# Batch 1's normalised input split in natural layout and turned by DMA; the first PSUM copies of batch 0 one weight part earlier

## The chip, the cores and the metric

The program runs on one core of one Trainium2 chip. The metric is the time of one execution on the device in microseconds (us): the median of the runs shown. One TensorE (PE), one VectorE (DVE), one ScalarE (ACT), one GpSimd (POOL) and one SyncE (SP) with its DMA queue take part. Every plain DMA of the kernel is issued by SP.

## The reference, cut to what matters

```python
x = L0_attn_x                                  # 2 x 1024 x 512, float32
xn = _layernorm(x, axis=-1)
q, k, v = proj(Wq), proj(Wk), proj(Wv)         # xn @ W.T, 16 heads of 32
scores = einsum(q, k) / sqrt(32), causal mask, softmax
s = (attn @ v) @ Wo.T
hidden = silu(xn @ W1.T) * (xn @ W3.T)         # 2048 wide
g = silu(fwht(hidden) @ W2.T)                  # Walsh-Hadamard along the last axis
out = x + s * g
```

## The kernel before, in words

The two batches run one after the other, each through `project`, `heads` and `tail`. Every engine's program is written out by hand, in its own order, and engines meet only through semaphores (`wait_ge`, `then_inc`). There is no scheduler: what stands in a function for an engine runs in that order on it.

float32 products are made of two parts, a high and a low one, so that each product is three matmuls (hi by hi, lo by hi, hi by lo; function `three`, L1585 to L1587, and L1617 for the first groups). In batch 0 the projections of q and k use parts in a rounded float32 form (`xt_hi`, `xt_lo`, `w_hi`, `w_lo`); the projection of v, the products with W1 and W3, and in batch 1 the projections of q and k too, use fp16 parts `x16_hi` and `x16_lo` (the trace calls them x_hi and x_lo), which hold 2048 times xn. They are laid out with the 512 features on partitions: [128, 4, 1024].

The normalised input `xb` [128 rows, 8 tiles, 512] is in natural layout. TensorE turns it: `transpose_xn(b, t)` (L1594) makes four transposes of 128x128 float32 for a tile of 128 rows, into a PSUM bank (`xt_bank(t)`: s0, s1 and the two banks of m). ACT then copies the bank to the high part (`xt` L879, `x16` L887), and DVE subtracts it from the bank for the low part (`xt` L1251, `x16` L1257). Eight tiles per batch, `t` 0 to 7.

`project(b)` on PE is `first_groups` (groups 0 and 1 of q, 24 matmuls), then groups 2 to 15 of q and k, each 12 matmuls of 512 columns, then 8 groups of v. Group `c` 0 reads tiles 0 to 3, group `c` 1 (from group 8 on) tiles 4 to 7. The first four tiles are transposed before the groups, tiles 4 to 7 after groups 4, 5 and 6 (`XT_AFTER`).

The down stage is the second half of `tail(b)`: for the 8 row tiles, `down(tp, i)` multiplies the hidden values of tile `2 * tp + i` with the transformed W2, 48 matmuls of 512 columns in two halves of 24 (`h` 0 and 1). A half can start when `h_lo_done[h]` says that its values are split. When PE has finished a half (`h_used[h]`), ACT makes the next tile's high part of it (`hidden_hi`, L1100) and DVE the low part (`hidden_lo`, L1487). After a tile's second half ACT and DVE finish the output rows (`gate` L1142, `finish` L1527 to L1534), SP stores them and loads the next rows of x. Between these, in batch 0, DVE makes the statistics and the normalisation of batch 1's input: `statistics` after places (0, 1) and (1, 1), `normalise` after (1, 0) and (2, 0), with `root` on ACT (`STATS_AT`, `NORM_AT`). Just before the last tile (7) of batch 0's down stage PE transposes tiles 0 to 3 of batch 1; ACT and DVE split Wq's four blocks and then these four tiles while PE is in that last tile.

At the start of batch 0, ACT splits the first three blocks of Wq, copies the four transposed tiles, and then splits the last block. PE's `first_groups` needs the high parts of all four tiles, then the low parts of all four.

Of the kernel before, what the change touches and what calls it, by code (L numbers as in the profile page):

```python
# [29 lines left out]
P = 128  # L30
# [3 lines left out]
KT = D // P  # L34
# [68 lines left out]
NORM_AT = [(1, 0), (2, 0)]  # L103

# [17 lines left out]
def build(nc, x, wq, wk, wv, wo, w1w3, w2, hadamard, out):  # L122
# [8 lines left out]
    with ctx:  # L131
# [105 lines left out]
        sb("room_after_g_lo0", [P, JT // 2, D], F16)  # L237
# [49 lines left out]
        x16_hi_done, x16_lo_done = sem("x16_hi_done"), sem("x16_lo_done")  # L287
        w13_scaled, w13_sum, w13_sum_ps, w13_scale_step, scan_in = sem("w13_scaled"), sem("w13_sum"), sem("w13_sum_ps"), sem("w13_scale_step"), [sem(f"scan_in{i}") for i in range(3)]
# [199 lines left out]
        def _(sp):  # L488
# [167 lines left out]
            def tail(b):  # L656
# [195 lines left out]
        def _(act):  # L852
# [28 lines left out]

            def x16(b, t):
                if b == 0:
                    act.wait_ge(xt_lo_done, t + 1)
                else:
                    act.wait_ge(xt_ps, b * NT + t + 1)
                act.activation(x16_hi[:, :, t * P:(t + 1) * P], xt_bank(t).rearrange("p (k c) -> p k c", k=KT),  # L887
                               ACT.Copy, scale=X_TOP).then_inc(x16_hi_done, 1)

            def project(b):  # L890
# [12 lines left out]
                if b == 0:  # L903
                    root(b, 0)
                    for i in range(KT - 1):
                        split_weight(b, i)
                    for t in range(TPC):
                        xt(b, t)
                    split_weight(b, KT - 1)
                for g in range(NQK):  # L910
# [6 lines left out]
                    for t in XT_AFTER.get(g, ()):  # L917
                        (xt, x16)[b](b, t)
# [177 lines left out]
            def tail(b):  # L1096
# [50 lines left out]
                for tp in range(NT // 2 - 1):  # L1147
                    for i in range(2):
                        hidden_hi(tp * 2 + (i + 1))
                        gate(tp, i)  # L1150
                        if b + 1 < B and (tp, i) in NORM_AT:
                            root(b + 1, NORM_AT.index((tp, i)))
                hidden_hi(NT - 1)
                gate(NT // 2 - 1, 0)
                if b + 1 < B:
# [4 lines left out]
                    for t in range(TPC):  # L1160
                        x16(b + 1, t)
# [17 lines left out]
        def _(dve):  # L1179
# [68 lines left out]
            def xt(b, t):  # L1248
# [3 lines left out]
                                  xt_hi[at].bitcast(F32), ALU.subtract).then_inc(xt_lo_done, 1)  # L1252

# [69 lines left out]
            def project(b):  # L1323
# [19 lines left out]
                for g in range(NQK):  # L1343
# [6 lines left out]
                    for t in XT_AFTER.get(g, ()):  # L1350
                        (xt, x16)[b](b, t)
# [131 lines left out]
            def tail(b):  # L1483
# [57 lines left out]
                for tp in range(NT // 2 - 1):  # L1541
                    for i in range(2):
# [4 lines left out]
                        if b + 1 < B and (tp, i) in NORM_AT:  # L1547
                            normalise(b + 1, NORM_AT.index((tp, i)))
                hidden_lo(NT - 1)
                finish(NT // 2 - 1, 0)  # L1550
                if b + 1 < B:
                    for i in range(KT):
                        split_weight(b + 1, i)
                    for t in range(TPC):
                        x16(b + 1, t)
# [25 lines left out]
        def _(pe):  # L1581
# [21 lines left out]
            def project(b):  # L1603
                def first_groups():

                    def products(g, p):
# [5 lines left out]
                        for kt in range(KT):  # L1612
# [19 lines left out]
                def group(g):  # L1632
# [5 lines left out]
                    if g < NQK:  # L1638
                        c, m, r = QK_GROUPS[g]
                        pe.wait_ge((xt_lo_done, x16_lo_done)[b], b * NT + (c + 1) * TPC)  # L1640
                        pe.wait_ge(split_lo, split_no(b, (m + 1) * KT))
                    else:
                        t = g - NQK
                        pe.wait_ge(wv_lo_done, (b + 1) * KT)
                        pe.wait_ge(x16_lo_done, x16_no(b, t))
# [17 lines left out]
                for g in range(2, NG):  # L1663
# [10 lines left out]
                    for t in XT_AFTER.get(g, ()):  # L1674
# [182 lines left out]
            def tail(b):  # L1857
# [73 lines left out]
                for tp in range(NT // 2):  # L1931
                    for i in range(2):
                        if b + 1 < B and tp * 2 + i == NT - 1:
                            pe.wait_ge(attn_done, (b + 1) * NT)
                            for t in range(TPC):
                                transpose_xn(b + 1, t)
# [44 lines left out]
```

## Time and profile before

| | us |
|---|---|
| median of 3 runs | 928.82 (928.81 to 930.75) |
| the profiled execution, its own time | 929.33 |
| its span in the trace | 927.6 |
| PE busy | 917.1 (99%), 6541 matmuls |
| DVE busy | 710.5 (77%) |
| ACT busy | 611.6 (66%) |
| POOL busy | 291.7 (31%) |
| DMA: 107.91 MB, share of 16 engines | 37.7% |
| granted TensorE clock | 0.999 |

The span runs from the first instruction to the last in the trace; the execution's own time is 1.7 us more. A matmul's record begins when it enters the array and lasts longer than the distance to the next one, so that distances between starts, not durations, say what a matmul costs PE. The batches divide the span so: batch 0's project to about 85 us, heads to 365, tail to 485 with its down stage from about 402 on; batch 1 from 485 on.

### The profile page before, as it was taken

Reading aid. Unit: us, or ns where it says so; the run is one execution under the profiler, and the core shown is the slowest. Engines: PE = TensorE matmul, PEld = TensorE weight load, DVE = VectorE, ACT = ScalarE, POOL = GpSimd, SP = SyncE. Lnnn points to the kernel's source line nnn. Section 1 sums busy time; section 2 is a strip of 40 time slices with the busy share of each in tenths; the row PEclk is TensorE's granted clock in tenths of the full one; section 3 lists DMA queues with packets and bytes.
Section 4 is the critical chain, followed back from the end, with each engine's and each line's share of the span. In section 5 each row is a group of like instructions: output and inputs, shape, how many; then the busy total and the mean of one; then the engine's idle time right before and its main releaser. Section 6 shows DMA issues by size and latency. Waiting matters only on the chain.

```text
span 927.6 us, 18915 instructions
## 1 busy us (share of the span) xinstructions
PE 917.1 (99%) x6541; PEld 528.1 (57%) x6541; DVE 710.5 (77%) x1413; ACT 611.6 (66%) x1281; POOL 291.7 (31%) x528
## 2 busy tenths in 40 slices
PE   8999999999999999999999999999999999999998
PEld 7864655665655656854444445555555555585445
DVE  7787999899899898766664569898989989843344
ACT  4558889998888877852443337788777887833231
POOL 1896664556556344000000002322323223310000
PEclk9999999999999999999999999999999999999999
DMA  9797356656346413672115411121211212150111
GB/s 292 277 254 257 104 156 171 177 143 163 107 120 168 125 48 99 232 256 84 46 57 176 134 38 42 47 75 42 82 41 58 64 41 65 46 205 23 46 46 46
DMA packets 64974, 107.91 MB, mean 116 GB/s; under 512 B 6640, under 2 KB 27760, under 8 KB 64368
## 3 DMA queue, kind: packets, MB, share of 16 engines
q1 hardware_dynamic: 64880, 106.72, 37.7%
q8 instruction: 52, 0.85, 0.4%
q14 instruction: 42, 0.34, 0.1%
HBM read 72.94 MB, written 33.55 MB: 115 GB/s over the span
## 4 chain that ended last, share of the span: by engine, by line
PE 71%; ACT 3%; DVE 2%; issue 1%; DMA 1%; POOL 0%; ACTq 0%; POOLq 0%; DVEq 0%
PE f L1801 25%; PE f L1586 7%; PE f L1585 7%; PE f L1587 7%; PE s L1758 5%; PE m L1738 3%; PE o L1776 3%; PE m L1881 3%; PE xs L1738 1%; PE o L1778 1%; PE m L1886 1%; DMA qk_st<-m_lo 1%; DVE p_lo L1417 1%; ACT stages L976 1%; PE s L1853 1%
## 5 line engine op out<-in xcount | busy, mean ns | idle before, releaser
L1417 DVE TENSOR_TENSOR p_lo<-stages,p_hi 128x512 f16<-128x512 f32 (+2 forms) x288 | 193.8, 681 | 22.1 <-ACT p_hi L986 21.2
L1801 PE MATMUL f<-x_hi,w_lo 128*128 128x512 f16 x512 | 194.6, 380 | 0.0
L1801 PE MATMUL f<-x_lo,w_hi 128*128 128x512 f16 x512 | 194.4, 380 | 0.0
L1801 PE MATMUL f<-x_hi,w_hi 128*128 128x512 f16 x512 | 193.9, 379 | 0.0
L986 ACT ACTIVATE p_hi<-stages 128x512 f16<-128x512 f32 (+2 forms) x288 | 160.2, 556 | 24.9 <-ACT stages L976 13.6
L777 POOL TENSOR_SCALAR_AFFINE_SELECT stages<-stages 128x128 f32<-128x128 f32 x192 | 68.3, 361 | 264.6 <-ACT stages L976 264.1
L1758 PE MATMUL s<-qk_st 98*128 98x512 f32 (+6 forms) x384 | 118.6, 383 | 1.2 <-ACT stages L976 0.3
L976 ACT ACTIVATE stages<-s,qk_back 128x512 f32<-128x512 f32 x144 | 88.2, 613 | 30.3 <-PE s L1758 29.5
L1400 DVE CUSTOM_DVE_ANT_0 m<-m,causal 128x1024 f32<-128x1024 f32 (+1 forms) x98 | 104.4, 1066 | 1.2 <-PE m L1738 1.2
L1100 ACT ACTIVATE h_hi<-hidden 128x1024 f16<-128x1024 f32 x32 | 33.9, 1058 | 95.8 <-PE f L1587 95.8
L1487 DVE TENSOR_TENSOR h_lo<-hidden,h_hi 128x1024 f16<-128x1024 f32 x32 | 39.2, 1224 | 75.1 <-ACT h_hi L1100 75.1
L1585 PE MATMUL f<-g_hi,h_hi 128*128 128x512 f16 (+1 forms) x256 | 95.4, 372 | 0.0
L1586 PE MATMUL f<-g_lo,h_hi 128*128 128x512 f16 (+1 forms) x256 | 95.3, 372 | 0.0
L1587 PE MATMUL f<-g_hi,h_lo 128*128 128x512 f16 (+1 forms) x256 | 95.3, 372 | 0.0
L976 ACT ACTIVATE stages<-s 128x512 f32<-128x512 f32 x144 | 75.5, 525 | 26.6 <-PE s L1758 25.7
L1738 PE MATMUL m<-qk_st 96*128 96x512 f32 (+7 forms) x256 | 79.4, 391 | 0.7 <-DVE mx L1400 0.7
L1801 PEld LDWEIGHTS f<-x_lo,w_hi 128*128 128x128 f16 x512 | 49.9, 97 | 52.3 <-issue 10.3
L1776 PE MATMUL o<-vparts,p_hi 128*128 128x65 f16 x1152 | 77.5, 190 | 0.1
L1801 PEld LDWEIGHTS f<-x_hi,w_lo 128*128 128x128 f16 x512 | 49.7, 97 | 47.3 <-issue 7.7
L1776 PEld LDWEIGHTS o<-vparts,p_hi 128*128 128x128 f16 x1152 | 71.7, 96 | 8.4 <-DVE p_lo L1417 0.2
L1778 PE MATMUL o<-vparts,p_lo 128*128 128x33 f16 x1152 | 76.2, 178 | 0.0
L1801 PEld LDWEIGHTS f<-x_hi,w_hi 128*128 128x128 f16 x512 | 50.5, 99 | 40.1 <-issue 3.7
(291 smaller groups left out, 1876.4 us busy)
## 6 DMA issues: line engine op xcount, KB each, us to landing
qk_st<-qk_parts SPq DMA_DIRECT2D x48, 256.0 KB, 4.6
w<-w1w SPq DMA_DIRECT2D x16, 512.0 KB, 4.3
scan<-w1w SPq DMA_DIRECT2D x12, 512.0 KB, 5.0
qk_st<-qk_parts SPq DMA_DIRECT2D x48, 128.0 KB, 2.6
wht_in<-w SPq DMA_DIRECT2D x4, 1024.0 KB, 10.9
qk_parts<-qk_hi SPq DMA_DIRECT2D x16, 256.0 KB, 3.2
qk_parts<-qk_lo SPq DMA_DIRECT2D x16, 256.0 KB, 4.9
w_butterflied<-wht_in SPq DMA_DIRECT2D x4, 1024.0 KB, 6.1
```

The lines of the kernel that those rows point to most:

```text
L976: act.activation(expd[q % NE][:, 0:end - need], SB[q % 2][:, 0, need - start:end - start], ACT.Exp, scale=1.0 if q < NH * NS else qk_back[ ...
L986: act.activation(p_hi[s][:], expd[q % NE][:, 0:end - need], ACT.Copy).then_inc(p_hi_done, 1)
L1400: dve.tensor_tensor_reduce(out=bank, in0=bank, in1=causal[:, S - width:S], scale=1.0, scalar=LOWEST, op0=ALU.add, op1=ALU.max, accum_out=m ...
L1417: dve.tensor_tensor(p_lo[s][:], expd[q % NE][:, 0:end - need], p_hi[s][:], ALU.subtract).then_inc(p_lo_done, 1)
L1585: pe.matmul(o, a_hi, b_hi, start=first, stop=False)
L1586: pe.matmul(o, a_hi, b_lo, start=False, stop=False)
L1587: return pe.matmul(o, a_lo, b_hi, start=False, stop=last)
L1738: mm = pe.matmul(bank[:, at:end], q[0:STACK, t * P:(t + 1) * P], k[0:STACK, at:end], start=True, stop=True)
L1758: pe.matmul(SB[q % 2][:, 0, 0:end - start], k_st[n // NH][n % NH % 3][0:STACK + 2, k * P:(k + 1) * P], q_st[n // NH][n % NH % 3][0:STACK + ...
L1776: pe.matmul(O[:, 0, first:first + VN], p_hi[s][:, at:at + P], v, start=k == 0 and t == c * TPC, stop=False, skip_group_check=True)
L1778: mm = pe.matmul(O[:, 0, first + DH:first + VN], p_lo[s][:, at:at + P], v[:, DH:VN], start=False, stop=t == k, skip_group_check=True)
L1801: mm = pe.matmul(F[m][:, 0, :], w, v, start=k == 0, stop=k == GMM - 1)
```

## The change

1. Batch 1's tiles are no longer transposed by PE, and its fp16 parts no longer made from PSUM. Instead ACT makes the high part in natural layout, `xn_hi` (`xn_high`), DVE the low part `xn_lo` (`xn_low`), and SP turns each with one transposing DMA of 128x512 fp16 into `x16_hi` and `x16_lo` (`turn_x16`): 16 such DMAs. Tiles 0 and 1 are made and turned after place (1, 1) of batch 0's down stage, 2 and 3 after (2, 0), 4 and 5 after (2, 1) (`TURN_AT`), 6 and 7 after the splits of Wq (`TURN_LAST`). The new buffers hold four tiles each, so that ACT waits for the turning of tiles 0 to 3 before it writes tile 4 (`x16_in[0]`).
2. In batch 0's start ACT splits two blocks of Wq ahead of its four copies instead of three, and PE goes through the hi-by-hi products of groups 0 and 1 block by block, in turn, before it asks for the low parts.

```diff
+TURN_AT = {(1, 1): (0, 1), (2, 0): (2, 3), (2, 1): (4, 5)}
+TURN_LAST = (6, 7)
+TURNED = 2 * TPC * 16
...
-        sb("room_after_g_lo0", [P, JT // 2, D], F16)
+        xn_hi = sb("xn_hi", [P, TPC, D], F16)
+        xn_lo = sb("xn_lo", [P, TPC, D], F16)
...
+                def turn_x16(t):
+
+                    sp.wait_ge(xn_lo_done, t + 1)
+                    for dst, src in ((x16_hi, xn_hi), (x16_lo, xn_lo)):
+                        sp.dma_start_transpose(dst[:, :, t * P:(t + 1) * P], src[:, t % TPC, :]
+                                               ).then_inc(x16_in[t // TPC], 16)
...
                     load_first(b + 1)
+                    sp.wait_ge(ffn_ps, (b + 1) * NH * GROUPS)
                 for tp in range(NT // 2 - 1):
                     for i in range(2):
                         store_y(tp, i)
                         load_x(tp * 2 + (i + 2), i)
+                        if b + 1 < B:
+                            for t in TURN_AT.get((tp, i), ()):
+                                turn_x16(t)
                 if b + 1 < B:
                     for i in range(5, NQ - 1):
                         load_weight(b + 1, i)
                 store_y(NT // 2 - 1, 0)
                 if b + 1 < B:
+                    for t in TURN_LAST:
+                        turn_x16(t)
                     store_y(NT // 2 - 1, 1)
...
+            def xn_high(t):
+
+                act.wait_ge(xn_done, NT + (t + 1))
+                if t >= TPC:
+                    act.wait_ge(x16_in[0], TURNED)
+                act.activation(xn_hi[:, t % TPC, :], xb[:, t, :], ACT.Copy, scale=X_TOP).then_inc(xn_hi_done, 1)
...
-                    for i in range(KT - 1):
+                    for i in range(2):
                         split_weight(b, i)
                     for t in range(TPC):
                         xt(b, t)
-                    split_weight(b, KT - 1)
+                    for i in range(2, KT):
+                        split_weight(b, i)
...
                         gate(tp, i)
                         if b + 1 < B and (tp, i) in NORM_AT:
                             root(b + 1, NORM_AT.index((tp, i)))
+                        if b + 1 < B:
+                            for t in TURN_AT.get((tp, i), ()):
+                                xn_high(t)
...
+            def xn_low(t):
+
+                dve.wait_ge(xn_hi_done, t + 1)
+                dve.scalar_tensor_tensor(xn_lo[:, t % TPC, :], xb[:, t, :], X_TOP, xn_hi[:, t % TPC, :],
+                                         ALU.mult, ALU.subtract).then_inc(xn_lo_done, 1)
...
                             normalise(b + 1, NORM_AT.index((tp, i)))
+                        if b + 1 < B:
+                            for t in TURN_AT.get((tp, i), ()):
+                                xn_low(t)
...
-                    for t in range(TPC):
-                        x16(b + 1, t)
+                    for t in TURN_LAST:
+                        xn_low(t)
...
-                    pe.wait_ge((xt_hi_done, x16_hi_done)[b], b * NT + TPC)
-                    products(0, 0)
-                    pe.wait_ge((xt_lo_done, x16_lo_done)[b], b * NT + TPC)
+                    if b == 0:
+                        pe.wait_ge(xt_hi_done, TPC)
+                    else:
+                        pe.wait_ge(x16_in[0], TURNED)
+                    for kt in range(KT):
+                        for g in range(2):
+                            products(g, 0, [kt])
+                    if b == 0:
+                        pe.wait_ge(xt_lo_done, TPC)
                     products(0, 1)
-                    products(1, 0)
                     products(1, 1)
...
-                        pe.wait_ge((xt_lo_done, x16_lo_done)[b], b * NT + (c + 1) * TPC)
+                        if b == 0:
+                            pe.wait_ge(xt_lo_done, (c + 1) * TPC)
+                        else:
+                            pe.wait_ge(x16_in[c], TURNED)
...
                             pe.wait_ge(attn_done, (b + 1) * NT)
-                            for t in range(TPC):
-                                transpose_xn(b + 1, t)
```

Where the diff cuts lines, ACT's and DVE's loops over `XT_AFTER` and PE's `transpose_xn` in them now run for batch 0 alone, and the last two tiles' `xn_high` stands on ACT where `x16` of four tiles stood.

On PE, at the border between tiles 6 and 7 of batch 0's down stage, before:

```order
L1587 MATMUL f<-g_hi,h_lo 128x512
L1594 MATMUL s<-ident,xb 128x128 x8
L1594 MATMUL m<-ident,xb 128x128 x8
L1585 MATMUL f<-g_hi,h_hi 128x512
L1586 MATMUL f<-g_lo,h_hi 128x512
```

The two L1594 rows (four tiles, 16 transposes) are gone now, and so are the three places with 4, 4 and 8 of them in batch 1's project; tile 7's matmuls follow on tile 6's.

On DVE, in the down stage from place (1, 1) to the splits of Wq, before:

```order
L1223 BN_STATS stats<-xb 128x6 x4
L1487 TENSOR_TENSOR h_lo<-hidden,h_hi 128x1024 x2
...
L1245 TENSOR_SCALAR xb<-xb,mv,rstd 128x512 x4
L1487 TENSOR_TENSOR h_lo<-hidden,h_hi 128x1024 x2
L1527 SCALAR_TENSOR_TENSOR y<-y,f 128x512
L1530 TENSOR_TENSOR y<-y,ctx_nat 128x512
L1534 SCALAR_TENSOR_TENSOR y<-y,g_back,x_in 128x512
L1487 TENSOR_TENSOR h_lo<-hidden,h_hi 128x1024 x2
```

and now (its own line numbers):

```order
L1250 BN_STATS stats<-xb 128x6 x4
L1284 SCALAR_TENSOR_TENSOR xn_lo<-xb,xn_hi 128x512 x2
L1520 TENSOR_TENSOR h_lo<-hidden,h_hi 128x1024 x2
...
L1272 TENSOR_SCALAR xb<-xb,mv,rstd 128x512 x4
L1284 SCALAR_TENSOR_TENSOR xn_lo<-xb,xn_hi 128x512 x2
L1520 TENSOR_TENSOR h_lo<-hidden,h_hi 128x1024 x2
L1560 SCALAR_TENSOR_TENSOR y<-y,f 128x512
L1563 TENSOR_TENSOR y<-y,ctx_nat 128x512
L1567 SCALAR_TENSOR_TENSOR y<-y,g_back,x_in 128x512
L1284 SCALAR_TENSOR_TENSOR xn_lo<-xb,xn_hi 128x512 x2
L1520 TENSOR_TENSOR h_lo<-hidden,h_hi 128x1024 x2
```

Three times, two low parts now stand ahead of the low part of the next hidden tile, on the engine that PE waits for at each half; on ACT two high parts stand in the same three places ahead of the next `h_hi`.

On PE, the first groups of batch 0, now:

```order
L1630 MATMUL m<-ident,xb 128x128 x8
L1637 MATMUL f<-ident 128x128 x6
L1653 MATMUL f<-xt_hi,w_hi 128x512
L1653 MATMUL o<-xt_hi,w_hi 128x512
...
L1653 MATMUL f<-xt_lo,w_hi 128x512 x4
L1653 MATMUL o<-xt_lo,w_hi 128x512 x4
L1653 MATMUL f<-xt_hi,w_lo 128x512 x4
L1653 MATMUL o<-xt_hi,w_lo 128x512 x4
```

where before four of `f<-xt_hi,w_hi`, four of `f<-xt_lo,w_hi` and only then four of `o<-xt_hi,w_hi` came: eight matmuls instead of four now stand ahead of the first that needs a low part.

## Rows read from the trace of the kernel before

**Rows 1.** The page: busy time and share of each engine.

```profile
PE 917.1 (99%) x6541; PEld 528.1 (57%) x6541; DVE 710.5 (77%) x1413; ACT 611.6 (66%) x1281; POOL 291.7 (31%) x528
```

**Rows 2.** 10 us of the down stage: length; busy PE, PEld, DVE, ACT, POOL; PEclk, DMA, GB/s.

```profile
460.00:470.00 10.00, 10.00 (x48) 4.47 (x46) 5.79 (x7) 4.09 (x4) 0.00 (x0) 1.00 0.11 31
```

**Rows 3.** Timeline of PE around the transposes: start us, us, engine, line, instruction, count.

```profile
472.62 0.38 PE L1587 MATMUL f<-g_hi,h_lo 128*128 128x512 f16 x1
472.83 1.04 PE L1594 MATMUL s<-ident,xb 128*128 128x128 f32 x8
473.71 1.04 PE L1594 MATMUL m<-ident,xb 128*128 128x128 f32 x8
474.58 0.38 PE L1585 MATMUL f<-g_hi,h_hi 128*128 128x512 f16 x1
474.80 0.38 PE L1586 MATMUL f<-g_lo,h_hi 128*128 128x512 f16 x1
...
500.70 0.38 PE L1587 MATMUL o<-x_hi,w_lo 128*128 128x512 f16 x1
500.92 0.60 PE L1594 MATMUL s<-ident,xb 128*128 128x128 f32 x4
501.35 0.38 PE L1585 MATMUL xs<-x_hi,w_hi 128*128 128x512 f16 x1
...
503.94 1.04 PE L1594 MATMUL m<-ident,xb 128*128 128x128 f32 x8
504.82 0.38 PE L1585 MATMUL f<-x_hi,w_hi 128*128 128x512 f16 x1
```

**Rows 4.** Timeline of PE at the start: the first groups, 24 matmuls to group 2.

```profile
12.43 1.19 PE L1617 MATMUL f<-xt_hi,w_hi 128*128 128x512 f32 x4
13.48 1.21 PE L1617 MATMUL f<-xt_lo,w_hi 128*128 128x512 f32 x4
...
18.19 0.39 PE L1585 MATMUL xs<-xt_hi,w_hi 128*128 128x512 f32 x1
18.42 0.39 PE L1586 MATMUL xs<-xt_lo,w_hi 128*128 128x512 f32 x1
```

**Rows 5.** Timeline of ACT and DVE at the start.

```profile
8.51 1.92 ACT L857 ACTIVATE w_hi<-stages 128x512 fp32r<-128x512 f32 x3 [0.35 <-DMA stages<-wq]
9.02 1.92 DVE L1245 TENSOR_SCALAR xb<-xb,mv,rstd 128x512 f32<-128x512 f32 x4
...
12.15 1.28 DVE L1251 TENSOR_TENSOR xt_lo<-m,xt_hi 128x512 fp32r<-128x512 f32 x2
12.24 0.65 ACT L857 ACTIVATE w_hi<-w 128x512 fp32r<-128x512 f32 x1
```

**Rows 6.** Timeline of DVE in the down stage.

```profile
449.55 1.21 DVE L1487 TENSOR_TENSOR h_lo<-hidden,h_hi 128x1024 f16<-128x1024 f32 x1
...
460.15 1.22 DVE L1487 TENSOR_TENSOR h_lo<-hidden,h_hi 128x1024 f16<-128x1024 f32 x1
...
477.37 2.07 DVE L1188 SCALAR_TENSOR_TENSOR w_lo<-stages,qk_scale,w_hi 128x512 f16<-128x512 f32 x3
```

**Rows 7.** Timeline of PE where the next half of the hidden values begins.

```profile
452.11 0.38 PE L1585 MATMUL f<-g_hi,h_hi 128*128 128x512 f16 x1
...
462.47 0.38 PE L1585 MATMUL f<-g_hi,h_hi 128*128 128x512 f16 x1
```

**Rows 8.** Timeline of ACT in the down stage.

```profile
465.04 0.69 ACT L1142 ACTIVATE y<-f,g_back 128x512 f32<-128x512 f32 x1
467.85 1.06 ACT L1100 ACTIVATE h_hi<-hidden 128x1024 f16<-128x1024 f32 x1 [2.12 <-PE f L1587]
...
475.44 1.95 ACT L859 ACTIVATE w_hi<-stages,qk_scale 128x512 f16<-128x512 f32 x3 [0.77 <-issue]
```

**Rows 9.** DMA issues: count, KB each, median us from issue to landing.

```profile
qk_parts<-qk_lo SPq DMA_DIRECT2D x16, 256.0 KB, 4.9
qk_parts<-qk_hi SPq DMA_DIRECT2D x16, 128.0 KB, 1.7
```

More of the change, by code:

```diff
@@ L287, in build @@
         x16_hi_done, x16_lo_done = sem("x16_hi_done"), sem("x16_lo_done")
+        xn_hi_done, xn_lo_done, x16_in = sem("xn_hi_done"), sem("xn_lo_done"), [sem(f"x16_in{i}") for i in range(NC)]
         w13_scaled, w13_sum, w13_sum_ps, w13_scale_step, scan_in = sem("w13_scaled"), sem("w13_sum"), sem("w13_sum_ps"), sem("w13_scale_step"), [sem(f"scan_in{i}") for i in range(3)]
@@ L880, in xt @@
                                ACT.Copy).then_inc(xt_hi_done, 1)
+            def xn_high(t):
[3 more added lines that the diff above has]
+                act.activation(xn_hi[:, t % TPC, :], xb[:, t, :], ACT.Copy, scale=X_TOP).then_inc(xn_hi_done, 1)
             def x16(b, t):
[L883 to L886, printed above, removed]
+                act.wait_ge(xt_lo_done, t + 1)
                 act.activation(x16_hi[:, :, t * P:(t + 1) * P], xt_bank(t).rearrange("p (k c) -> p k c", k=KT),
@@ L916, in project @@
                         root(b, 1)
-                    for t in XT_AFTER.get(g, ()):
-                        (xt, x16)[b](b, t)
+                    if b == 0:
+                        for t in XT_AFTER.get(g, ()):
+                            xt(b, t)
                     if g - 1 in WV_AT:
@@ L1159, in tail @@
                         split_weight(b + 1, i)
-                    for t in range(TPC):
-                        x16(b + 1, t)
+                    for t in TURN_LAST:
+                        xn_high(t)
                 if b + 1 < B:
@@ L1349, in project @@
                         normalise(b, 1)
-                    for t in XT_AFTER.get(g, ()):
-                        (xt, x16)[b](b, t)
+                    for t in XT_AFTER.get(g, ()) if b == 0 else ():
+                        xt(b, t)
                     for t in X16_AFTER.get(g, ()) if b == 0 else ():
@@ L1553, in tail @@
                         split_weight(b + 1, i)
-                    for t in range(TPC):
-                        x16(b + 1, t)
+                    for t in TURN_LAST:
+                        xn_low(t)
                 if b + 1 < B:
@@ L1604, in first_groups, with products @@
                 def first_groups():
-                    def products(g, p):
+                    def products(g, p, kts=range(KT)):
                         r = QK_GROUPS[g][2]
@@ L1611, in products @@
                             w, v = (w16_hi, w16_hi, w16_lo)[p][0], (x16_hi, x16_lo, x16_hi)[p]
-                        for kt in range(KT):
+                        for kt in kts:
                             if g == 0 and p == 0:
@@ L1644, in group @@
                         pe.wait_ge(wv_lo_done, (b + 1) * KT)
-                        pe.wait_ge(x16_lo_done, x16_no(b, t))
+                        if b == 0:
+                            pe.wait_ge(x16_lo_done, x16_no(b, t))
                     for kt in range(KT):
@@ L1673, in project @@
                     group(g)
-                    for t in XT_AFTER.get(g, ()):
+                    for t in XT_AFTER.get(g, ()) if b == 0 else ():
                         transpose_xn(b, t)
@@ L1934, in tail @@
                             pe.wait_ge(attn_done, (b + 1) * NT)
-                            for t in range(TPC):
-                                transpose_xn(b + 1, t)
                         if b + 1 == B and tp * 2 + i == NT - 1:
```

1 line of the change is left out of this document (added).

## The prediction

> **What bounds the kernel.** I read the page's first part, then busy time by stretches, then the timelines of single engines at the places that the change touches. TensorE is busy 917.1 of 927.6 us [rows 1], and in the down stage, where most of the change lies, all 10.00 of 10.00 us at full clock, with DVE, ACT (5.79 and 4.09 us) and the DMA engines (0.11) mostly free [rows 2]. So whatever leaves TensorE's program shortens the kernel by its own time, as long as no other engine then comes late at one of TensorE's waits. The reader should see two things: what a row costs TensorE is the distance between starts, 0.22 us for a matmul of 512 columns [rows 3], and the waits that can come late are those for `h_lo`, since DVE and ACT get new work ahead of them.
>
> **Part 1, what is removed from TensorE.** Four tiles stood between 472.83 and 474.58, after a matmul begun at 472.62. From there to 474.58 are 1.96 us, of which 0.22 belong to the matmul: 1.74 us for 16 transposes [rows 3]. A place with four of them costs 501.35 - 500.70 - 0.22 = 0.43 us, and there are two of these (after groups 4 and 5; the other reads the same); the place with eight costs 504.82 - 503.94 = 0.88 us [rows 3]. The sum is 1.74 + 2 x 0.43 + 0.88 = 3.48 us. The 16 copies by ACT and subtractions by DVE from PSUM go with them, and 16 of like size from SBUF come: ACT about 0.65 us each and DVE about 0.66 us each, by the split of Wq with the same types (1.95 and 2.07 us for three) [rows 6, 8].
>
> **Where they come, DVE.** Twice two low parts, 1.32 us, go in front of an `h_lo` half that TensorE wants soon. At place (1, 1) `h_lo` began at 449.55 and took 1.21 us; with 1.32 us more it ends at 452.08. The half's first matmul began at 452.11, and its weight load, which is what waits, about 0.1 us ahead of it: TensorE comes some 0.1 us late [rows 6, 7]. At (2, 0), 460.15 + 1.32 + 1.22 = 462.69 against 462.47: 0.2 us, with the load's lead and some 0.05 us for the semaphore 0.4 us late [rows 6, 7]. Together I take +0.5 us; the ends are 0 (if operands from SBUF go at half that time) and +1.3 us (if each low part costs a quarter more, which adds 0.33 us in each of the two places). At (2, 1) and after the splits of Wq the pieces have microseconds to spare. On ACT the high parts at (1, 1) and (2, 0) are ahead of DVE's own chain and cost nothing.
>
> **Part 1, the transposing DMAs.** The trace of before has none, so their cost is bounded. What hides them is the down stage's 10.4 us per tile. The tight one is ACT's wait for the turning of tiles 0 to 3 before it writes tile 4, since ACT then owes TensorE the next `h_hi`. Tiles 2 and 3 are ready to be turned at 460.15 + 1.32 = 461.5 (tile 2 a little before) [rows 6]. TensorE wants tile 7's first half at 472.7, where it used to begin the transposes [rows 3]. Back from there: `h_lo` 1.21, `h_hi` 1.06, two high parts 1.3: the four DMAs must have landed by 469.1, 7.6 us after 461.5 [rows 3, 6, 8]. ACT itself is free from 465.7 [rows 8]. The nearest rows are DMAs of the same 128 KB, 1.7 us from issue to landing, and as the other end 4.9 us for 256 KB [rows 9]. At the first figure even four in series need 6.8 us and just fit, and in part they will overlap. I take this as the likeliest, as equal in bytes and on idle DMA engines [rows 2]: cost 0. The other end is the slower rival. SP's queue has nothing else to do there but stores and loads of rows that are needed a tile later; the transposing DMAs of tiles 6 and 7 are needed only at group 8, some 20 us after the down stage, and the last block of Wk, behind them in the queue, when group 4 begins.
>
> The Trainium skill (DMA: Bandwidth & Descriptors, Latency and other measured facts) gives transposing DMAs an effective 261 GB/s; by that figure 128 KB is an estimated 0.5 us of transfer, which would make the cost 0 as well. No row here shows it.
>
> **Part 2, the start.** The 24 matmuls of the first groups last from 12.43 to 18.19, 5.76 us; at the 0.23 us that one takes right after them they would last 5.44 us [rows 4]. The other 0.32 us is the wait for the low parts, which DVE ends at 12.15 + 1.28 = 13.43, just before the fifth matmul at 13.48 [rows 4, 5]. With eight matmuls ahead of it, 1.8 us of work from 12.4, the low parts are ready first: -0.32 us. The copies themselves can gain little: with one split less (8.51 + 1.92 for three) [rows 5] ACT is free at about 9.8, but the tiles come out of DVE's normalisation only from 9.5 on and one each 0.46 us until 10.94, and must still be transposed. I take -0.08 us. The two late splits follow the copies at about 12.9 and 13.5 and meet TensorE's third and fourth pair at 13.3 and 13.7: 0. Part 2: -0.4 us, bounds 0 and -0.7 us.
>
> **The sum.** -3.48 + 0.5 - 0.4 = -3.4 us. The profiled execution took 929.33 us, so it would take 925.9; it lies 0.5 us above the median of the runs, 928.82, which becomes **925.4 us**. All later work of both batches starts that much earlier and its waits are between engines that move together, so I cost it at nothing.
>
> **Rivals.**
>
> The gain is half eaten by ACT's wait (0.13). If the DMAs are served one after another at 2.5 us each, the fourth of tiles 2 and 3 lands at 461.5 + 10.0 = 471.5, 2.4 us after 469.1, and TensorE stands at tile 7's first half for 2.4 us: 927.8 us. For it: issue and landing of all of them go through one queue, and 256 KB took 4.9 us where stores were dense [rows 9]. Against: DMA engines are 0.11 busy here [rows 2].
>
> Slower (0.19): the transposing DMA is a slow kind of DMA, and the series of eight holds ACT, and by it `h_hi` and TensorE, in front of tile 7. It loses the whole gain when tiles 2 and 3 take 7.6 + 3.4 = 11.0 us, that is from 2.8 us per DMA on. At 4.9 us each in series [rows 9] eight of them last 39.2 us from 450.9 (449.55 + 1.32) and land at 490.1, 21.0 us late; tiles 4 to 7 then land at 530.6, and group 8 of batch 1, due 20.7 us after a down stage that ends at 504, waits another 6: 928.8 - 3.4 + 27 = 952 us. For it speaks only that the trace holds no such DMA to disprove it; against it, that the bytes are few.
>
> The Trainium skill (VectorE: DVE Perf Modes, The three transpose paths) speaks against the change: 1309 ns for a DMA transpose of one 128x128 block of two-byte values against 390 ns on TensorE, and it says to take TensorE when PSUM will do. If a DMA of four blocks costs four times that, an estimated 5.2 us, the sum above would give some 958 us. On TensorE this trace has 0.11 us per transpose, so the work moved is smaller still than the page has it.
>
> Smaller effects of the start, such as a gain there that is lost again at a later wait, stay within the forecast's own span.
>
> **How the numbers follow.** Forecast 0.68, half eaten 0.13, slower 0.19. A measurement of this kernel can tell about 0.2%, 1.9 us, from no change, so faster means under 926.96. The forecast's own span is 924.6 (no late `h_lo`, the start's full 0.7: -4.2) to 926.9 (1.3 us of late `h_lo` and nothing at the start: -2.2, rounded up), and lies in faster: 0.68. The half-eaten case spans 927.0 to 930.7: same, 0.13. Slower: 0.19. The range, 924.2 to 930.0, takes the forecast with 0.4 us below for the runs' scatter and most of the second case, leaving out the slow rival, which is nearly 2 in 10 and open upwards.
>
> **What the changed profile would show.** No transposes from xb on TensorE after 35 us, and tile 7's first matmul about 0.22 us after tile 6's last. TensorE idle for under 1 us in all in the down stage, released by `h_lo`, at the halves that follow places (1, 1) and (2, 0). Landing times of the transposing DMAs near 2 us, and ACT's high part of tile 4 begun straight after its gate at about 465.5. Group 2 of batch 0 begun at about 17.8 instead of 18.19. I am wrong if ACT's first high part of tile 4 begins after 469, if PE idles before tile 7 on ACT or DVE, or if batch 1's groups wait for a transposing DMA.

## The result and the profile after

The changed kernel took 926.38 us (median of 5 runs, 925.41 to 926.91), the kernel before 930.75 us (5 runs, 928.81 to 930.83); the ratio is 0.995, 95% interval 0.9935 to 0.9964. A later series on another occasion gave 926.4 us against 930.02, ratio 0.9953 (0.9937 to 0.9969). The forecast was 925.4 us, in a range from 924.2 to 930.0, and faster with a chance of 0.68. It was reckoned from 928.82 us, the median of three runs of the kernel before, where the five give 930.75: the median after lies 1.0 us above the forecast, and the difference of the medians is 4.4 us where 3.4 was forecast.

The profiled execution took 925.41 us, its span is 923.7 us against 927.6. The page of the kernel after, busy time of the engines, against [rows 1]:

```profile
PE 912.8 (99%) x6509; PEld 524.6 (57%) x6509; DVE 709.9 (77%) x1413; ACT 611.0 (66%) x1281; POOL 290.8 (31%) x528
```

TensorE has 32 matmul instructions less and 4.3 us less busy time; ACT and DVE have as many instructions as before. TensorE is still busy for 99% of a shorter span.

TensorE's timeline after the change, at the half that follows place (2, 0) and at the border between tiles 6 and 7 (start us, us, engine, line, instruction):

```profile
461.36 0.38 PE L1623 MATMUL f<-g_hi,h_lo 128*128 128x512 f16 x1
461.82 0.38 PE L1621 MATMUL f<-g_hi,h_hi 128*128 128x512 f16 x1
...
471.96 0.38 PE L1623 MATMUL f<-g_hi,h_lo 128*128 128x512 f16 x1
472.18 0.38 PE L1621 MATMUL f<-g_hi,h_hi 128*128 128x512 f16 x1
```

Where 1.96 us lay between two matmuls of the down stage [rows 3], 0.22 us lie now. The one new place of the down stage where the distance is larger than 0.22 us is 461.36 to 461.82, 0.46 us: DVE's low part of the next hidden tile comes 0.24 us late. (One more, at the start of the stage, stands in both kernels, 1.14 us before and 1.16 after.) The half after place (1, 1) is not late. DVE in front of the late half:

```profile
459.25 1.29 DVE L1284 SCALAR_TENSOR_TENSOR xn_lo<-xb,xn_hi 128x512 f16<-128x512 f32 x2
460.46 1.22 DVE L1520 TENSOR_TENSOR h_lo<-hidden,h_hi 128x1024 f16<-128x1024 f32 x1
```

The DMA issues of the kernel after (count, median us to landing) and SP's queue with ACT beside it after place (2, 0):

```profile
x_hi<-xn_hi SPq DMA_TRANSPOSE x8, 2.8
x_lo<-xn_lo SPq DMA_TRANSPOSE x8, 2.5
```

```profile
459.97 1.20 SPq L692 DMA_TRANSPOSE x_hi<-xn_hi  x1
461.21 1.26 SPq L692 DMA_TRANSPOSE x_lo<-xn_lo  x1
462.52 1.26 SPq L692 DMA_TRANSPOSE x_hi<-xn_hi  x1
463.82 1.27 SPq L692 DMA_TRANSPOSE x_lo<-xn_lo  x1
```

```profile
464.14 0.69 ACT L1166 ACTIVATE y<-f,g_back 128x512 f32<-128x512 f32 x1
466.41 1.15 ACT L905 ACTIVATE xn_hi<-xb 128x512 f16<-128x512 f32 x2 [1.57 <-DMA x_lo<-xn_lo]
467.46 1.04 ACT L1124 ACTIVATE h_hi<-hidden 128x1024 f16<-128x1024 f32 x1
```

A transposing DMA lands 2.5 to 2.8 us (medians) after its issue begins. 14 of the 16 hold SP's queue for 1.20 to 1.33 us, the other two (at 452.02 and 480.09) for 2.03 and 2.46 us; the stores and loads of rows beside them hold it 0.34 to 0.43 us. So the four of tiles 2 and 3 go out one behind the other, and ACT, whose gate ends at 464.8, waits 1.57 us for the last of them. TensorE does not feel it. Reckoned back from 471.97, where the load of tile 7's first weights begins, over `h_lo` (1.22), `h_hi` (1.04) and two high parts (1.05), ACT may begin as late as about 468.6; it began at 466.41.

TensorE's timeline at the start, after the change, against [rows 4]:

```profile
9.37 1.04 PE L1630 MATMUL s<-ident,xb 128*128 128x128 f32 x8
...
12.12 0.50 PE L1653 MATMUL f<-xt_hi,w_hi 128*128 128x512 f32 x1 [0.19 <-ACT xt_hi L897]
12.46 0.40 PE L1653 MATMUL o<-xt_hi,w_hi 128*128 128x512 f32 x1
...
14.10 1.08 PE L1653 MATMUL f<-xt_lo,w_hi 128*128 128x512 f32 x4
...
17.74 0.39 PE L1621 MATMUL xs<-xt_hi,w_hi 128*128 128x512 f32 x1
```

Group 2 begins at 17.74 instead of 18.19, but the first transpose of `xb` too begins 0.25 us earlier (9.37; before 9.62), because the last tiles of x arrived earlier in this execution (before, DVE waits 1.04 us for them between its statistics of the tiles, and after it does not). From the first transpose to group 2 it is 8.37 us instead of 8.57. The 24 matmuls take 5.62 us instead of 5.76.

Read by stretches between fixed instructions of TensorE (differences of starts in the timelines), the two kernels compare so:

| stretch | before, us | after, us | difference |
|---|---|---|---|
| first transpose of xb to group 2 of batch 0 | 8.57 | 8.37 | -0.20 |
| group 2 to the first matmul of the down stage | 381.18 | 380.71 | -0.47 |
| down stage to the first group of batch 1 | 85.57 | 84.09 | -1.48 |
| first group to the first group of v, batch 1 | 43.19 | 41.44 | -1.75 |
| v and the first scores, batch 1 | 25.40 | 25.40 | 0 |
| first scores to the last of the down stage, batch 1 | 369.51 | 369.77 | +0.26 |

With the 0.25 us by which the first transpose is earlier these make the 3.9 us by which the spans differ. The experiments say which of them belong to the change: -0.20, -1.48 and -1.75.

### The profile page after: what moved, and what is told of

The parts are those of the page before. It is cut to its first block, busy times and chain, and to the rows that moved or that the text cites. A ratio compares the mean times of both kernels' runs of the same rounds, so it can differ in the third digit from the quotient of the medians.

```text
span 923.7 us, 18867 instructions
## 1 busy us (share of the span) xinstructions
PE 912.8 (99%) x6509; PEld 524.6 (57%) x6509; DVE 709.9 (77%) x1413; ACT 611.0 (66%) x1281; POOL 290.8 (31%) x528
## 4 chain that ended last, share of the span: by engine, by line
PE 77%; DVE 4%; ACT 2%; issue 1%; DMA 1%; POOL 0%; SPq 0%; ACTq 0%; POOLq 0%; DVEq 0%
PE f L1846 29%; PE f L1621 7%; PE f L1623 7%; PE f L1622 7%; PE s L1803 6%; PE m L1783 4%; PE o L1821 4%; PE m L1926 3%; PE xs L1783 2%; PE o L1823 2%; PE m L1931 1%; DVE p_lo L1450 1%; DMA w<-wo 1%; ACT stages L1000 1%; PE s L1898 1%
```

## The experiments

All edits are against the kernel named; every one keeps the whole computation unless the text says otherwise.

### One part alone

`start_only`, the kernel before with the start changed:

```diff
-                    for i in range(KT - 1):
+                    for i in range(2):
                         split_weight(b, i)
                     for t in range(TPC):
                         xt(b, t)
-                    split_weight(b, KT - 1)
+                    for i in range(2, KT):
+                        split_weight(b, i)
...
-                    products(0, 0)
+                    for kt in range(KT):
+                        for g in range(2):
+                            products(g, 0, [kt])
                     pe.wait_ge((xt_lo_done, x16_lo_done)[b], b * NT + TPC)
                     products(0, 1)
-                    products(1, 0)
                     products(1, 1)
```

> The kernel before with the start alone changed: two splits of Wq ahead of the copies instead of three, and the hi-by-hi products of groups 0 and 1 block by block in turn. My sum says -0.4 us: group 2 begins 0.4 us earlier after the first transpose of xb on TensorE (8.57 us from 9.62 to 18.19 before, so about 8.2), and the whole time is 0.3 to 0.5 us less. Rival: the start is set by the arrival of x and by the 33 transposes that keep TensorE busy, so that the distance from the first transpose of xb to group 2 shrinks by 0.2 us at most and nothing of it is seen in the whole time (within 0.2 us).

Measured: 929.65 us (12 runs) against 931.0 (35 runs), ratio 0.9986 (0.9969 to 1.0003): not told from no change. From the first transpose to group 2 it is 8.43 us (9.52 to 17.95). The stretches of batch 1 are those of the kernel before: 85.58 and 43.18 us. The start gives 0.14 us by this trace. The rival was right about its size, less than half of my 0.4 us. In all eight traces with both edits of the start this distance lies between 8.34 and 8.43 us.

`turn_only`, the changed kernel with both places of the start put back as they were:

> The changed kernel with the start of the kernel before, so the turning by DMA alone. If the parts add up, 3.48 - 0.24 (one late h_lo) = 3.2 us below the kernel before, about 0.4 us above the changed kernel. Rival: the two parts interact (the earlier start is what makes the later waits shorter), then it is more than 0.8 us above the changed kernel. In the trace the distance from tile 7's last matmul in the down stage to tile 6's first is 1.74 us shorter than before.

Measured: 927.36 us (12 runs), ratio 0.9964 (0.9951 to 0.9978), which does not overlap 1. Down stage to batch 1's first group 84.06 us, from there to v 41.44 us, as in the changed kernel; first transpose to group 2 8.62 us, as before. Stretch by stretch the parts add up, and this is what speaks against an interaction. The medians do not: 927.36 lies 1.0 us above the changed kernel (926.38 and 926.4 in two other series), which by the letter of the expectation is on the rival's side of 0.8 us. The intervals of the ratios overlap (0.9951 to 0.9978 here, 0.9935 to 0.9964 and 0.9937 to 0.9969 there), so whole times of different series decide nothing at this size.

`start_pe`, the kernel before with TensorE's new order of the first groups alone (the second hunk above):

> The kernel before with TensorE's order of the first groups alone changed; ACT still makes three splits first. From the first transpose of xb to group 2 it took 8.57 us before and 8.35 to 8.43 us with both edits of the start. The theory that the wait for the low parts was worth 0.14 us (one matmul begun 0.34 instead of 0.23 us before its next) says 8.43 to 8.45. Rival: the gain comes from ACT's earlier copies, then it stays at 8.55 to 8.6.

TensorE's timeline of this kernel:

```profile
9.47 1.11 PE L1594 MATMUL s<-ident,xb 128*128 128x128 f32 x8 [1.08 <-DVE xb L1245]
...
12.41 0.50 PE L1617 MATMUL f<-xt_hi,w_hi 128*128 128x512 f32 x1 [0.26 <-ACT xt_hi L879]
12.75 0.39 PE L1617 MATMUL o<-xt_hi,w_hi 128*128 128x512 f32 x1
...
17.99 0.39 PE L1585 MATMUL xs<-xt_hi,w_hi 128*128 128x512 f32 x1
```

The distance is 8.52 us, between the two expectations. The 24 matmuls take 5.58 us, 0.18 less than before; the first of them begins 2.94 us after the first transpose (2.81 in the kernel before, 2.90 in `turn_only`). Over all traces the 24 matmuls take 5.76 and 5.72 us in the old order and 5.58 to 5.62 in the new one, so TensorE's order gives about 0.15 us. The first of them begins 2.81, 2.90 and 2.94 us after the first transpose where ACT still makes three splits first, and 2.75 to 2.81 in the eight traces with two: the earlier copies give 0 to 0.2 us, some 0.1 by the means, and three traces on the one side do not fix it better. The first matmul after a pause keeps its successor 0.34 us away instead of 0.23 (12.41 to 12.75). In the kernel before, the fifth of the 24, the first that needs a low part, has such a distance of 0.34 us too; in the new order none but the first has it.

### TensorE's transposes put back

`pe_back`, the changed kernel with the 32 transposes of batch 1 on TensorE again. Their results are not read, and the fp16 parts still come by DMA:

```diff
+            def turn_unread(t):
+                pe.wait_ge(xn_done, NT + t + 1)
+                for kt in range(KT):
+                    pe.transpose(xt_bank(t)[:, kt * P:(kt + 1) * P], xb[:, t, kt * P:(kt + 1) * P], ident[:])
...
-                    for t in XT_AFTER.get(g, ()) if b == 0 else ():
-                        transpose_xn(b, t)
+                    for t in XT_AFTER.get(g, ()):
+                        (transpose_xn if b == 0 else lambda _, t: turn_unread(t))(b, t)
...
                             pe.wait_ge(attn_done, (b + 1) * NT)
+                            for t in range(TPC):
+                                turn_unread(t)
```

> The changed kernel with the 32 transposes of batch 1 put back on TensorE in their four old places, their results unread. The theory that the gain is TensorE's own time says +3.48 us on the changed kernel (span about 927.2 against 923.7), and 1.74 us of it between tiles 6 and 7. Rival: part of the gain came from ACT and DVE work that no longer waits for PSUM banks; then the transposes give back clearly less than 3.4 us, say 2.5.

Measured: 930.05 us (12 runs), ratio 0.9982 (0.9968 to 0.9995). The two stretches are 85.81 us (84.09 + 1.72) and 43.19 us (41.44 + 1.75): 3.47 us come back, 0.01 us from the price of [rows 3]. TensorE between tiles 6 and 7:

```profile
473.32 0.38 PE L1623 MATMUL f<-g_hi,h_lo 128*128 128x512 f16 x1
473.54 1.04 PE L1637 MATMUL s<-ident,xb 128*128 128x128 f32 x8
474.41 1.04 PE L1637 MATMUL m<-ident,xb 128*128 128x128 f32 x8
475.28 0.38 PE L1621 MATMUL f<-g_hi,h_hi 128*128 128x512 f16 x1
```

ACT and DVE still work from SBUF here, so the rival of a gain from freed ACT and DVE falls. The profiled execution of this kernel was its slowest, 933.05 us; a wait of TensorE, 0.3 us in the kernel before, is most of the reason (engine, line, waited for: total us, times, longest):

```profile
PE s L1808 <- DMA qk_st<-m_lo: 3.3, 5, 0.8
```

It is a wait of the heads for the DMA that puts the maxima into the stack of q. The last section comes back to it.

### How late the turning may be

`turn_more`, the changed kernel with four more transposing DMAs:

```diff
-TURNED = 2 * TPC * 16
+TURNED = [(2 * TPC + 4) * 16, 2 * TPC * 16]
...
-                    for dst, src in ((x16_hi, xn_hi), (x16_lo, xn_lo)):
+                    for n, (dst, src) in enumerate(((x16_hi, xn_hi), (x16_lo, xn_lo))):
+                        if t in (2, 3):
+                            at = (2 * (t - 2) + n) * D
+                            sp.dma_start_transpose(unread[:, at:at + D].rearrange("p (k c) -> p k c", k=KT),
+                                                   src[:, t % TPC, :]).then_inc(x16_in[0], 16)
```

> The changed kernel with four more transposing DMAs, beside those of tiles 2 and 3, into room that nobody reads; ACT's wait counts them. A transposing DMA holds SP's queue 1.27 us. The theory of the queue says: eight of them from 460.0 end their issue at 470.2, the last lands 1.3 us later at 471.5, ACT may begin tile 4's high part at 468.6 at the latest, so TensorE stands 2.9 us before tile 7 and the time is 2.7 to 3.1 us above the changed kernel. Rival: the 1.27 us are overlapped in some way (the DMAs run side by side and only the row of the queue is long), then ACT is released at about 467 to 468 and the time is unchanged.

Measured: 931.94 us (12 runs), ratio to the kernel before 1.0007 (0.9992 to 1.0022): the whole gain is gone. SP, ACT and TensorE:

```profile
460.37 1.21 SPq L694 DMA_TRANSPOSE room_after_g_lo<-xn_hi  x1
...
469.46 1.27 SPq L696 DMA_TRANSPOSE x_lo<-xn_lo  x1
```

```profile
472.04 1.15 ACT L909 ACTIVATE xn_hi<-xb 128x512 f16<-128x512 f32 x2 [6.80 <-DMA x_lo<-xn_lo]
473.10 1.99 ACT L1128 ACTIVATE h_hi<-hidden 128x1024 f16<-128x1024 f32 x2
```

```profile
475.54 0.59 PE L1625 MATMUL f<-g_hi,h_hi 128*128 128x512 f16 x1 [2.80 <-DVE h_lo L1524]
```

The queue is serial: eight DMAs from 460.37 end their issue at 470.73, ACT goes on at 472.04, and TensorE stands 2.80 us before tile 7, where 2.9 was expected. But the stretch is 88.67 us, 4.58 more than 84.09, not 2.9. TensorE by windows (stretch, length, busy time and count, granted clock, DMA share, GB/s) has the rest:

```profile
472.00:474.00 2.00, 0.74 (x4) 1.00 0.81 236
474.00:476.00 2.00, 0.46 (x2) 0.87 0.35 71
476.00:478.00 2.00, 2.00 (x6) 0.50 0.63 126
478.00:480.00 2.00, 2.00 (x9) 0.77 0.33 66
```

The granted clock falls to 0.50, which is 1.2 instead of 2.4 GHz, as the pause ends and stays there until about 479. The first matmul has its successor 0.38 us away and the next seven 0.43 us instead of 0.22: 1.6 us more. With the pause itself (3.18 us between two starts, 0.22 of them usual) that is 4.6 us. No expectation of mine for this run had this; the next one, written after it, has. The chain from ACT's start at 472.04 to TensorE's at 475.54 takes 3.50 us, which puts the latest harmless start of ACT in the changed kernel at 472.18 - 3.50 = 468.7, as reckoned.

### What holds the queue

`turn_halves`, each transposing DMA cut in two of 128x256:

```diff
-TURNED = 2 * TPC * 16
+TURNED = 4 * TPC * 16
...
-                        sp.dma_start_transpose(dst[:, :, t * P:(t + 1) * P], src[:, t % TPC, :]
-                                               ).then_inc(x16_in[t // TPC], 16)
+                        for k in range(0, KT, 2):
+                            sp.dma_start_transpose(dst[:, k:k + 2, t * P:(t + 1) * P], src[:, t % TPC, k * P:(k + 2) * P]
+                                                   ).then_inc(x16_in[t // TPC], 16)
```

> The changed kernel with each transposing DMA cut in two of 128x256, 32 in all. If SP's queue is held for each 128x128 block, a half takes some 0.64 us and nothing else changes: ACT waits 1.6 us for tile 4 as now. Rival: it is held for each DMA, 1.27 us whatever the size; then eight of them after place (2, 0) last 10.2 us, ACT waits until about 471.5, and TensorE stands about 2.9 us before tile 7 and loses some 1.8 us more at the halved clock that follows.

Measured: 937.8 us in its one run. Rows of its SP queue, of ACT, and two of TensorE's waits:

```profile
462.81 2.47 SPq L693 DMA_TRANSPOSE x_hi<-xn_hi  x2
465.32 2.53 SPq L693 DMA_TRANSPOSE x_lo<-xn_lo  x2
...
499.32 0.43 SPq L499 DMA_DIRECT2D stages<-wk  x1
```

```profile
474.20 1.15 ACT L906 ACTIVATE xn_hi<-xb 128x512 f16<-128x512 f32 x2 [7.99 <-DMA x_lo<-xn_lo]
```

```profile
PE f L1622 <- DVE h_lo L1521: 4.0, 1, 4.0
...
PE f L1622 <- DVE w_lo L1216: 2.6, 1, 2.6
```

Half the size, the same time in the queue: 2.53 us for two. The rival holds: the queue is held for each DMA. Two places now pay. Before tile 7 TensorE stands 4.0 us, where 2.9 was expected: the eight DMAs of tiles 0 and 1 hold the queue until 461.7, so that those of tiles 2 and 3 begin at 462.81, later than the expectation had them, and ACT is released at 474.20. Then the last block of Wk, whose load stands in the queue behind the DMAs of tiles 6 and 7, is issued at 499.32 (487.18 in the changed kernel), its low part comes late, and group 4 of batch 1 stands 2.6 us. Both pauses are followed by matmuls 0.43 us apart, twelve after the first and six after the second. This kernel has one run, but what it is read for, the queue and the pauses, is in its trace.

`low_between`, the changed kernel with DVE's low parts between the halves of the next hidden tile:

```diff
-                        hidden_lo(tp * 2 + (i + 1))
+                        hidden_lo(tp * 2 + (i + 1), (0,))
+                        for t in late:
+                            xn_low(t)
+                        hidden_lo(tp * 2 + (i + 1), (1,))
                         finish(tp, i)
...
-                        if b + 1 < B:
-                            for t in TURN_AT.get((tp, i), ()):
-                                xn_low(t)
+                        late = TURN_AT.get((tp, i), ()) if b + 1 < B else ()
-                hidden_lo(NT - 1)
+                hidden_lo(NT - 1, (0,))
+                for t in late:
+                    xn_low(t)
+                hidden_lo(NT - 1, (1,))
```

> The changed kernel with DVE's two low parts moved from ahead of the next tile's first h_lo half to between its two halves, where DVE stands idle 1.2 to 1.5 us for ACT. The theory that the only late h_lo is the one after place (2, 0) says: the extra 0.24 us between TensorE's matmuls at about 461.4 is gone and the whole time is 0.24 us less. The low parts come 1.2 us later, so the last transposing DMA of tiles 2 and 3 lands at about 467.6 instead of 466.4; the limit of 468.6 is still kept. Rival: that margin is not there, ACT's wait then reaches TensorE before tile 7 and the time is up to 1 us more.

Measured: 926.47 us (12 runs), ratio 0.9955 (0.994 to 0.997). The base of this series was the changed kernel again, `after_again`:

> The changed kernel once more, on the same chip as the next three, as their base. From its first runs: 926.4 us, 0.45% below the kernel before.

It took 926.4 us (10 runs). The down stage's stretch is 84.09 us in `after_again` and 83.84 us in `low_between`: the 0.25 us are there, as expected, and too small to be seen in whole times. ACT goes on at 469.14, 2.71 us late, in an execution whose stages lay 1.6 us later than in the first profile of the changed kernel, and TensorE does not wait for it: the margin held.

`one_per_tile`, `low_between` with both parts of a tile side by side and turned by one DMA of 128x1024:

```diff
-TURNED = 2 * TPC * 16
+TURNED = TPC * 16
...
-            x16_hi = sb("x16_hi", [P, KT, S], F16, r)
-            x16_lo = sb("x16_lo", [P, KT, S], F16, r)
+            x16_both = sb("x16_both", [P, 2 * KT, S], F16, r)
+            x16_hi, x16_lo = x16_both[:, 0:KT, :], x16_both[:, KT:2 * KT, :]
...
-        xn_hi = sb("xn_hi", [P, TPC, D], F16)
-        xn_lo = sb("xn_lo", [P, TPC, D], F16)
+        xn = sb("xn", [P, TPC, 2 * D], F16)
+        xn_hi, xn_lo = xn[:, :, 0:D], xn[:, :, D:2 * D]
...
-                    for dst, src in ((x16_hi, xn_hi), (x16_lo, xn_lo)):
-                        sp.dma_start_transpose(dst[:, :, t * P:(t + 1) * P], src[:, t % TPC, :]
-                                               ).then_inc(x16_in[t // TPC], 16)
+                    sp.dma_start_transpose(x16_both[:, :, t * P:(t + 1) * P], xn[:, t % TPC, :]
+                                           ).then_inc(x16_in[t // TPC], 16)
```

> The kernel with the low parts between the h_lo halves, and hi and lo parts of a tile side by side, so that one transposing DMA of 128x1024 turns both: 8 in all, the same bytes. If SP's queue is held 1.27 us for each DMA whatever its size, as the halves showed (1.24 us), two of them after place (2, 0) last 2.5 us, the second lands 1.3 us later, and ACT's wait before tile 4 (1.6 us in the changed kernel, 2.7 us with the low parts between) is gone. TensorE waits for none of this in either kernel, so the whole time stays within 0.5 us of 926.4. Rival: above 128x512 the queue is held by the size, 2.5 us for one DMA; then ACT's wait stays at about 2.7 us.

```profile
463.06 2.62 SPq L691 DMA_TRANSPOSE x_both<-xn  x2
```

```profile
467.58 1.15 ACT L904 ACTIVATE xn<-xb 128x512 f16<-128x512 f32 x2 [0.79 <-DMA x_both<-xn]
```

Measured: 926.75 us (7 runs), ratio 0.9958 (0.994 to 0.9975), no difference to the changed kernel, as expected. Two DMAs of twice the size hold the queue 2.62 us, 1.31 each, and land 3.2 us (median) after their issue. ACT's wait shrinks from 2.71 to 0.79 us. It was expected to be gone; a DMA of twice the size lands some 0.65 us later (3.15 us after its issue for this one, 2.50 for the one of 128x512), which the expectation did not count. The rival, a queue held by size above 128x512, falls. Neither variant beats the changed kernel by more than runs can tell; this one holds the queue for half as long.

## Why the prediction was right

**The bound.** "Whatever leaves TensorE's program shortens the kernel by its own time" held: the predicted 3.48 us for the 32 transposes [rows 3] came back as 3.47 us when they were put back.

**Late low parts.** I took +0.5 us, 0.1 after (1, 1) and 0.4 after (2, 0). It was 0 and 0.24 us. The low parts were cheaper than the 0.66 us taken from Wq's split: two of them shift the next piece by 1.19 to 1.21 us instead of 1.32 (448.64 to 449.83 and 459.25 to 460.46 on DVE), and these 0.1 us are all of the first term and most of what the second has too much. The later place was right, the earlier one was not late, and the term was twice too large.

**The turning.** The cost of 0 was right, the reason only in part. I took 1.7 us from issue to landing by the plain DMA of the same 128 KB [rows 9], and "even four in series need 6.8 us". They took 6.4 us from the first issue to ACT's start (459.97 to 466.41). What makes them serial is SP's queue, held 1.27 us for each; the landing is 2.5 to 2.8 us. That the queue could be the limit stood only in the half-eaten rival, by another row. So the change fitted with 2.2 us to spare (466.41 against about 468.6), but my reckoning of the room had the wrong latency and the wrong reason for the series, and that both errors left the cost at 0 is in part luck. One sign that I had named did not come: ACT's high part of tile 4 was to begin straight after its gate, and waited 1.57 us.

**The start.** I took -0.4 us, of which -0.32 for the wait for the low parts. That was mis-sized: the traces with both edits give -0.14 to -0.23, -0.20 in the changed kernel. I had counted the whole excess of the 24 matmuls over 5.44 us as that wait. After the change the excess is still 5.62 - 5.44 = 0.18 us, of which 0.11 us is the longer distance after the first matmul (0.34 instead of 0.23) and 0.07 us is spread over the others. The wait for the low parts was worth one more such distance of 0.34 us and a few hundredths of a microsecond.

**The sum.** -3.4 us was forecast for the two parts together. The stretches that belong to the change give -0.20 - 1.48 - 1.75 = -3.43 us: two terms were off, the start by +0.20 us and the late low parts by -0.26, and cancelled. That the sum came out to 0.05 us is luck; the 3.48 us were not. The medians differ by more, 4.4 and 3.6 us in the two series, with intervals that reach from 2.9 to 6.0 us. `pe_back`, which by the stretches should be level with the kernel before (-0.20 for the start, +0.24 for the late half), has a median 1.0 us below it and an interval (0.9968 to 0.9995) that leaves out 1. The likely source is the scatter: 15 of the 35 executions of the kernel before in that series took over 932 us, and 2 of 12 of `start_only`, none of 12 of `turn_only` and 1 of 12 of `pe_back`. Whether the change has a part in this was not tried, so of the medians' difference only the 3.4 us of the stretches are shown. The kernel before scattered from 928.4 to 935.7 over all series, and the 0.47 us of batch 0's heads in the table are nothing that the change did: `start_only`, `turn_only` and `after_again` have 380.19, 380.97 and 381.01 us in that stretch.

**The rivals.** The half-eaten and the slow one had the right place: ACT's wait for tiles 2 and 3, in front of tile 7. `turn_more` shows it at work. Their limit, 469.1 in the time of the kernel before, was about right (468.6 in that of the changed kernel, whose stages lie 0.9 us earlier: 469.5). Their price was too low: I priced a late landing at one us for each us, and the pause of 2.8 us cost 4.6, because the clock fell to half behind it. I had the whole gain, 3.4 us, lost when the turning of tiles 2 and 3 lands 11.0 us after DVE has made their parts. In `turn_more` the last of its eight DMAs lands just so late (DVE's parts are ready at 460.94, the landing is at 471.96), and the stretch lost 4.6 us, more than all of it.

The Trainium skill (VectorE: DVE Perf Modes) gives 1309 ns for a DMA transpose of one block (The three transpose paths) and advises TensorE when PSUM will do (Rules for kernel authors). No run here has a DMA of one block. That of four blocks lands in 2.5 to 2.8 us and that of eight in 3.2, so the time does not grow in proportion to the blocks, and the estimate of 958 us, which let it, did not come. Against the advice, the 32 transposes cost 3.2 us less as DMAs (the stretches -1.48 and -1.75), on a kernel whose TensorE is busy 99% of the time.

## What to carry to other kernels

When TensorE is busy 99% of the time, small work on it has a price that can be read from the distances between its starts, and moving it to a path with more latency pays, as it did here, as long as the chain back from TensorE's next wait has room: work that chain out backwards and keep the margin in view. Count a transposing DMA as time in the queue of the engine that issues it, and move more with each: up to 128x1024 the time in the queue hardly grew here. A pause of TensorE can cost more than itself: the three of 2.6, 2.8 and 4.0 us in `turn_more` and `turn_halves` were each followed by matmuls at half the clock.

## What the runs showed of the hardware that I had not expected

A transposing DMA held SP's queue for about the same time at the three sizes tried: 1.24 us for 128x256, 1.27 us for 128x512, 1.31 us for 128x1024 values of two bytes; landing took 2.4, 2.5 to 2.8 and 3.2 us (medians). In every trace one or two of them held it longer, 1.8 to 2.5 us; why was not tried.

Pauses of TensorE of 2.59 us (before group 4 in `turn_halves`) and 2.80 us (`turn_more`) ended with the granted clock at 0.50, and matmuls 0.43 us apart followed, in `turn_more` until about 479. The Trainium skill (TensorE: Matmul & The Clock Gate, What's actually happening) has these same two levels, 1.2 and 2.4 GHz, and the trace agrees (0.43 against 0.22 us for 512 columns).

The scatter between executions of one kernel, up to 7 us here, lies in the traces largely in one place of the heads: TensorE's wait for the small DMA of the maxima. Its total in four profiles, in the order `turn_only` (926.05 us), `after_again` (927.9), `turn_more` (933.94) and `start_pe` (933.99):

```profile
PE s L1801 <- DMA qk_st<-m_lo: 0.2, 1, 0.2
```

```profile
PE s L1803 <- DMA qk_st<-m_lo: 1.8, 5, 0.6
```

```profile
PE s L1807 <- DMA qk_st<-m_lo: 3.6, 6, 0.9
```

```profile
PE s L1759 <- DMA qk_st<-m_lo: 4.4, 7, 0.9
```

`start_pe` differs from the kernel before only in the order of the first groups' matmuls and took 4.7 us more than the profiled execution of that kernel, with 4.1 us more of this wait (0.3 us there). A single time of this kernel therefore says little, and a stretch between two instructions in the trace says much: the two stretches around batch 1's start repeat to 0.03 us over the kernels that have them alike. It is the landing that is late, not the issue: in batch 1 SP issues each of these DMAs 0.03 us after DVE has written the maxima, in the kernel before, in `turn_more` and in `start_pe` alike, and in `start_pe` TensorE's next matmul of the kind starts 2.71 us after the issue in most cases and 3.3 to 3.8 us after it in the four with a wait. Why it lands late in some executions was not tried.
